# Reordering the opening of a fused attention and mixture-of-experts layer: weight loads, first scores, output-weight folding and the transposes' queue

## The reference, cut to what matters

```python
q_latent = hidden_states @ Wqa
q = (q_latent @ Wqb).reshape(b, s, H, Q_HEAD_DIM)
kv_comp = hidden_states @ Wkva
c_kv, k_pe = (kv_comp[..., :KV_LORA], kv_comp[..., KV_LORA:])
...
kv = (c_kv @ Wkvb).reshape(b, s, H, NOPE_DIM + V_DIM)
scores = jnp.einsum('bhqd,bhkd->bhqk', q_full, k_full) * scale
probs = jax.nn.softmax(jnp.where(causal, scores, min), axis=-1)
attn = jnp.einsum('bhqk,bhkd->bhqd', probs, v)
x = x + attn.reshape(b, s, H * V_DIM) @ Wo
...
y = jnp.einsum('eti,eih,te->th', swiglu(x @ w_gate_up), w_down, combine)
x = x + y + swiglu(x @ shared_gate_up) @ shared_down
```

## Time and profile before

| what | value |
|---|---|
| runs | 1592.03, 1595.13, 1594.93 us |
| the profiled execution | 1592.03 us, of which 1589.2 us is the span of its instructions |
| PE busy | 1463.6 us (92%) |
| DVE / ACT / POOL busy | 1210.4 / 1009.7 / 988.4 us (76 / 64 / 62%) |
| mean granted TensorE clock | 0.982 of full |
| DMA | 144.66 MB, mean 91 GB/s |

### The profile page before, as it was taken

One profiled execution on the slowest core, in us unless ns is written; L12 is line 12 of the kernel. 1 busy time (PEld: TensorE's weight loads), 2 busy tenths in 40 slices (PEclk: granted clock), 3 DMA queues, 4 the chain that ended last, 5 costly groups with the idle time before them and its releaser, 6 DMA issues.

```text
span 1589.2 us, 44790 instructions
## 1 busy us (share of the span) xinstructions
PE 1463.6 (92%) x16413; PEld 1082.6 (68%) x16414; DVE 1210.4 (76%) x2657; ACT 1009.7 (64%) x2399; POOL 988.4 (62%) x1567
## 2 busy tenths in 40 slices
PE   9879999998899999998999999989999999979990
PEld 3557777776667777776677777766777767657770
DVE  6877778987778887877777778877777788556666
ACT  3666667666567666765676667666666666547770
POOL 4477755452878556576878678758786582444450
PEclk9999999999999999999999999999999999989995
DMA  7456933313554331234543123254532311448518
GB/s 214 83 113 162 167 71 67 60 20 71 100 104 74 71 61 31 50 66 84 109 88 71 35 53 65 46 93 78 99 64 42 65 27 31 107 126 249 148 58 320
DMA packets 331075, 144.66 MB, mean 91 GB/s; under 512 B 278546, under 2 KB 321589, under 8 KB 330872
## 3 DMA queue, kind: packets, MB, share of 16 engines
q1 hardware_dynamic: 305296, 104.57, 33.0%
q10 hardware_dynamic: 18664, 20.52, 4.5%
q0 software_dynamic: 6912, 16.83, 3.5%
HBM read 47.04 MB, written 29.53 MB: 48 GB/s over the span
## 4 chain that ended last, share of the span: by engine, by line
PE 70%; DVE 9%; ACT 6%; DMA 5%; issue 4%; SPq 1%; another core or an unknown queue 1%; POOL 1%; ACTq 0%; DVEq 0%; POOLq 0%
PE of_ps L772 28%; PE s_ps L772 25%; PE t_ps L969 15%; DMA qT<-work 3%; DVE pT L1828 2%; ACT probs L1304 2%; ACT pT L1179 1%; ACT work L1182 1%; DVE smax L1801 1%; DVE weights L2037 1%; PE of_ps L1094 1%; PE t_ps L1080 1%; DMA work<-y_exp 1%; DVE work L1625 1%
## 5 line engine op out<-in xcount | busy, mean ns | idle before, releaser
L1828 DVE TENSOR_TENSOR pT<-t_ps,pT 128x512 f16<-128x512 f32 (+3 forms) x688 | 411.0, 598 | 146.6 <-ACT pT L1179 138.4
L1179 ACT CAST pT<-t_ps 128x512 f16<-128x512 f32 (+3 forms) x688 | 355.6, 517 | 239.3 <-PE t_ps L969 238.5
L772 PE MATMUL s_ps<-kT,qT 128*128 128x512 f16 (+3 forms) x2112 | 473.0, 336 | 4.0 <-DMA qT<-work 4.0
L969 PE MATMUL t_ps<-id,probs 128*128 128x128 f32 x2304 | 378.7, 279 | 22.3 <-ACT probs L1304 8.5
L969 PEld LDWEIGHTS t_ps<-id,probs 128*128 128x128 f32 x2304 | 256.9, 141 | 105.9 <-issue 46.4
L772 PEld LDWEIGHTS of_ps<-ckv,pT 128*128 128x128 f16 x6912 | 241.0, 98 | 41.3 <-DVE o_sb L1657 9.5
L772 PE MATMUL of_ps<-ckv,pT 128*128 128x64 f16 x6912 | 257.8, 193 | 7.1 <-DVE o_sb L1657 6.5
L772 PEld LDWEIGHTS s_ps<-kT,qT 128*128 128x128 f16 x2112 | 202.8, 98 | 72.7 <-DMA qT<-work 4.9
L1304 ACT ACTIVATE probs<-s_ps,nmax 128x640 f32<-128x640 f32 (+3 forms) x256 | 245.9, 961 | 0.1
L772 PE MATMUL of_ps<-weights,xT 128*128 128x128 f16 (+1 forms) x930 | 198.0, 349 | 19.0 <-DVE work L1625 8.6
L1790 DVE TENSOR_REDUCE nmax<-s_ps 128x1 f32<-128x640 f32 (+3 forms) x200 | 192.4, 962 | 17.4 <-PE s_ps L772 16.9
(11 more groups left out here) (243 smaller groups left out, 2352.6 us busy)
## 6 DMA issues: line engine op xcount, KB each, us to landing
wgu_sb<-wgu ACTq DMA_DIRECT2D x8, 704.0 KB, 5.1
work<-lists SPq DMA_DIRECT2D x40, 128.5 KB
qT<-lists SPq DMA_DIRECT2D x40, 128.5 KB
x<-x SPq DMA_DIRECT2D x32, 128.0 KB
dense<-den SPq DMA_DIRECT2D x32, 128.0 KB
weights<-dense ACTq DMA_DIRECT2D x1, 4096.0 KB
qT<-y_exp SPq DMA_DIRECT2D x16, 256.0 KB, 6.4
work<-y_exp SPq DMA_DIRECT2D x16, 256.0 KB, 8.2
```

Of the source, the lines that this page charges most:

```text
L772: return pe_.matmul(o, a, b, start=start, stop=stop)
L969: last = pe_.transpose(t_ps[:, h, c * P:(c + 1) * P], probs[:, u % 2, g * L + j * P:g * L + (j + 1) * P], id32[:, :])
L1179: return act.copy(o, i)
L1828: dve.tensor_tensor(pT[:, u % 2, 1, h, 0:w], t_ps[:, h, 0:w], pT[:, u % 2, 0, h, 0:w], ALU.subtract).then_inc(s.lo_p, 1)
```

## The change

1. Loads and semaphores: the semaphore `consts` is gone; its seven loads and those of the cosine and sine tables count one semaphore `c_in`. SP issues the loads in the same order as before.
2. ACT issues the loads of `wvT` and `wo` at its start, as soon as the weights counted by `w_k` have landed, and not after the transposes of input tiles 0 and 1.
3. `constants()` moves on DVE from the end of `row_bounds()` to behind `query_lo(0, 0)`; DVE's own wait for the tables ahead of `latent_lo(0)` is gone.
4. PE: `fold_out(0)`, a wait for `c_ready`, three `busy_id` and the first unit of tile 0's scores come ahead of `project(0, "q1")`; `fold_out(1)` comes behind it and `fold_out(2)` behind `project(1, "q1")`; six `busy_id` instead of four stand ahead of the second unit of scores. The output weights' banks are 2, 2, 0, 0 and not 2, 0, 2, 0, with waits to match.
5. ACT: `out_weights(0)` moves ahead of `rope_hi(1)` and `query_hi(0, 1)`, `out_weights(1)` between the last two `query_hi`, `out_weights(2)` ahead of the first exponentials. DVE: `maxima(0, 0)` moves behind `query_lo(1, 1)`.
6. SP: the transposes are issued in the order keys 0, queries (0, 0), (0, 1), keys 1, queries (1, 0), (1, 1), first keys. Before, the first keys stood third, between the halves of tile 0's queries.

```diff
-        OUT_BANKS = [2, 0, 2, 0]
+        OUT_BANKS = [2, 2, 0, 0]
...
+            dest_in = dest_f[:, :]
             for dst, src in ((id32[:, :], ident), (probs[:, 1, 0:P], causal), (probs[:, 0, 0:P], tri),
                              (iota_e_sb[:, :], iota_e), (iota_k_sb[:, :], iota_k), (iota_p_sb[:, :], iota_p),
-                             (dest_f[:, :], tok_ids)):
-                load(dst, src, s.consts)
-            load(r_nopeT, wqb_nopeT, s.w_k)
-            load(r_wkT, wkT, s.w_k)
-            load(cos_sb[:, :, :], cos_t, s.c_in)
-            load(sin_sb[:, :, :], sin_t, s.c_in)
+                             (dest_in, tok_ids), (cos_sb[:, :, :], cos_t), (sin_sb[:, :, :], sin_t)):
+                load(dst, src, s.c_in)
+                if dst is dest_in:
+                    load(r_nopeT, wqb_nopeT, s.w_k)
+                    load(r_wkT, wkT, s.w_k)
...
-            turn_keys(0)
-            turn_half_queries(0, 0)
+            for n in range(2):
+                turn_keys(n)
+                for g in range(2):
+                    turn_half_queries(n, g)
             turn_first_keys(0)
-            turn_half_queries(0, 1)
-            turn_keys(1)
-            turn_half_queries(1, 0)
-            turn_half_queries(1, 1)
...
             project(1, "q0", 0, 512)
+            fold_out(0)
+            pe_.wait_ge(s.c_ready, 1)
+            busy_id(s_ps[:, 0, :], 3)
+            for h in range(2):
+                scores(0, 0, h)
             pe_.wait_ge(s.lo_made, FIRST)
             project(0, "q1", 512, 512)
-            pe_.wait_ge(s.c_ready, 1)
-            for h in range(2):
-                scores(0, 0, h)
+            fold_out(1)
             project(1, "q1", 512, 512)
-            for pair in range(3):
-                fold_out(pair)
-            busy_id(s_ps[:, 3, :], 4)
+            fold_out(2)
+            busy_id(s_ps[:, 3, :], 6)
             for h in range(2):
                 scores(0, 1, h)
+
+            pe_.wait_ge(s.wo_copied, 3)
             fold_out(3)
-
-            pe_.wait_ge(s.wo_copied, 3)
...
             copy(den[:, 0:1], pT[:, 0, 0, 0, 0:1])
+
+            act.wait_ge(s.w_k, 16 * 2)
+            load(r_wvT, wvT, s.w_o)
+            load(r_wo, wo.rearrange("(h d) n -> d h n", d=VD), s.w_o)
...
-            for k in range(2):
-                act.wait_ge(*x_turned(k))
-            load(r_wvT, wvT, s.w_o)
-            load(r_wo, wo.rearrange("(h d) n -> d h n", d=VD), s.w_o)
...
+            out_weights(0)
+            rope_hi(1)
             query_hi(0, 1)
-            rope_hi(1)
             query_hi(1, 0)
+            out_weights(1)
             query_hi(1, 1)
-            out_weights(0)
-            out_weights(1)
+            out_weights(2)
             exps(0, 0, 0)
-            out_weights(2)
...
-                dve.wait_ge(s.consts, 16 * 7)
+                dve.wait_ge(s.c_in, 16 * 9)
...
                 dve.sem_inc(s.rows_ready, 1)
-                constants()
...
-            dve.wait_ge(s.c_in, 16 * 2)
             latent_lo(0)
...
             query_lo(0, 0)
+            constants()
             lo_parts(7, 8)
...
             query_lo(1, 0)
-            maxima(0, 0)
             query_lo(1, 1)
...
             dve.sem_inc(s.side_free, len(OPENING))
+            maxima(0, 0)
             maxima(0, 1)
```

More of the change, by code:

```diff
@@ L271, in build @@
         s_flat = s_ps[:, :, :].rearrange("p a n -> p (a n)")
-        names = """c_in consts w_k w_a0 w_a1 w_o w_kv w_b filled c_ready qb_made qb_copied wq_made wo_made wo_copied prep
+        names = """c_in w_k w_a0 w_a1 w_o w_kv w_b filled c_ready qb_made qb_copied wq_made wo_made wo_copied prep
                    rows_ready row_sums amax_ready scales hi_made lo_made w_d
@@ L822, in fold_out @@
                     pe_.wait_ge(s.w_o, 16 * 2)
-                if pair < 2:
+                if pair % 2 == 0:
                     k = OUT_BANKS[pair]
@@ L827, in fold_out @@
                 else:
-                    pe_.wait_ge(s.wo_copied, pair - 1)
+                    pe_.wait_ge(s.wo_copied, pair)
                 bank = early_banks[OUT_BANKS[pair]]
```

## The result

The changed kernel takes 1603.37 us, the median of five runs (1602.24 to 1605.74), against 1592.42 us (1591.05 to 1595.13) for the kernel before beside it. The ratio is 1.0069, with a 95% interval of 1.0052 to 1.0087: slower by 11 us. The profiled execution took 1604.73 us with a span of 1602.6, 13.4 us more than the span before.

A forecast was written before the change was run, and what follows sets the result against it. PE was taken to bound the kernel (busy 92% of the span, heading the chain). Terms 2.4 + 2.4 + 3.1 = +7.9 us, added to the three-run mean of 1594.1, gave 1602 us; range 1596 to 1607.

The forecast's parts named there:

- the forecast's own path: Opening of the kernel: parts 2, 3 and 4 add 2.4, 2.4 and 3.1 us, giving 1602 us; chance 0.42.
- the third rival, the lowered clock: PE behind the longer stalls: two new 3 us stalls may each bring half clock, +2.6 to +5 us on top; chance 0.10.
- three signs of being wrong: Input tile 0 lands in under 3 us; last transposes drain faster than SP's 5.67 us for two; other low clock stretches.
- Part 1: Semaphores and moved constants() on DVE: nothing, as the later project(0, "q1") hides it; without that cover 0.5 us.
- Part 2: ACT's early output-weight loads slow input tile 0's transpose, PE stalls 3.2 us, project(0, "q0") starts +2.4 us later.
- The rival of packets taking turns: Input tile 0's transpose beside the early load: landing after 4.3 us, +0.6 instead of +2.4 us; load-slows-little chance 0.25.
- The -0.8 us end of part 2: Lower end with an undisturbed transpose: rotary path and DVE's split 0.9 us earlier, PE uses its gap, -0.8 us.
- Part 3: PE's new order, query half 1 later: 1.5 us wait ahead of tile 0's second scores, section(0) +2.4 us.
- Part 4: First keys last on SP: they land at about 57, PE stalls ahead of tile 1's first scores, +3.1 us.
- the fourth rival: Half-speed stretch at 70 us goes as work arrives in another rhythm: its price is 2.6 us, at most 3.4; chance 0.09.

The follow-up runs named there:

- half load: Kernel before with wvT and the first half of wo (1.5 MB) loaded at ACT's start, the second half in the old place; ratio 1.0000.
- late loads: Changed kernel with the loads of wvT and wo back behind the first two input transposes; ratio 1.0054, median 1600.42 against 1593.35.
- single edits: Kernel before with early loads (1.0028, 1.0029) or first keys last (1.0021); changed kernel with loads and SP's order as before (1.0036).
- filling the gaps: Changed kernel with unread matmuls, 18 ahead of the first projection and 12 ahead of tile 1's first scores; ratio 1.0061.

## Why the prediction was right, point by point

Forecast were +7.9 us for the profiled opening and 1602 us; measured were 12.2 us up to the projection of tile 2, 11 us between the medians, and 1603.4 us. The time was met more closely than the shift, and that is luck: the 7.9 us were added to a mean of 1594.0 us over three runs (the prediction wrote 1594.1), and the kernel before came to 1592.42 beside the changed one. What ran was the forecast's own path and, on top of it, the third rival, the lowered clock, which had been given 0.10: 7.9 + 3.8 = 11.7 us, against 12.2 in the trace. Of the three signs of being wrong that the prediction named one did come, low stretches of the clock that the kernel before does not have (0.53 from 25 to 30 us).

- **Part 1, constants at nothing:** right for this change, where the split they delay has its cover (no gap ahead of `project(0, "q1")` in the changed kernel). The price without the cover was mis-sized: 0.5 us forecast, 1.8 us more gap in the trace and 2.9 us in time, since in its new place the work takes twice as long (3.3 us and 1.6).
- **Part 2, +2.4 us:** the mechanism was right, the term was mis-sized, 5.6 us in the trace. Two of its numbers failed. The landing was taken at 6.1 us as an upper bound and was 7.2: tile 2's transpose had been issued between the two loads (22.39, with `wvT` at 22.34 and the 2 MB of `wo` at 22.70), and tile 0's stood behind both. This cost little, since the transpose was also issued 0.7 us earlier than taken: the first projection began at 23.93 and not 23.4. And the gap was thought to cost only itself; instead the clock fell behind it, and from the first projection to `project(0, "q0")` it took 13.5 us and not 10.7, which is the 2.8 us. That stood among the rivals with a chance of 0.10.
- **The rival of packets taking turns** (a landing of 4.3 us, +0.6): refuted by the queues' packets and by landings that follow the load whenever the transpose was issued; the half load's 0.7 us would have fitted it. The Trainium skill's rule ("DMA: Bandwidth & Descriptors", queues, rings and completion order) describes the engines once both queues have packets there, and after 21 us the rows do show both. What it does not cover is that the transpose's packets came to the engines only when less than a quarter of the load ahead was left; which stage before the engines holds them is not shown by any run.
- **The -0.8 us end of part 2**, the gap ahead of `project(0, "q0")` closed by a freer ACT: not shown. Several kernels have no such gap whatever ACT does.
- **Part 3, +2.4 us:** 2.4 in the changed kernel (8.1 less 5.6), 2.9 with late loads. Right, though two small errors cancel: the gap ahead of the second scores was 1.08 us where 1.5 was forecast, and PE's work from `project(0, "q1")` up to it 6.3 us where 5.9 was.
- **Part 4, +3.1 us:** 3.1 (11.2 less 8.1), a gap of 2.96 us, released by the first keys. Right, and alone it is 2.1. The prediction's own terms (54.5 + 2.4 against 54.0) give 2.9, and not the 3.1 that it wrote.
- **The lowered clock, +2.6 to +5:** it came in addition to the forecast, 2.8 and 1.0 us. The prediction gave them a case of their own. But the three longest gaps (4.24, 3.98 and 2.96 us) were each followed by a stretch of half clock, so with stalls as long as forecast the fall belonged into the forecast. Below that the length of the gap does not decide: 2.21 us, and gaps of 1.85, 2.37 and 2.39 us ahead of the first fold, were followed by a mean granted clock of 0.51 to 0.74, gaps of 1.97 and 1.98 us, and one of 2.29 us ahead of the first fold, were not, and the same 2.14 us were four times out of twelve.
- **The half-speed stretch at 70 us that might go** (the fourth rival): it did not. In the changed kernel it stands from about 88 us (0.60 in 88 to 92, 0.57 in 70 to 78 before), and from tile 2's projection to the first `weights,oT` product it took 22.2 us and 21.8 before.

The single edits cost 0.28 to 0.29%, 0.21% and 0.36% by themselves, 0.85 together, against 0.69% for the whole, within the intervals. What was not shown: why the profiled span ends 13.4 us later and not 12.2 (other stretches of half clock come and go between executions); that undoing part 2 or part 4, or filling the gaps, makes the changed kernel faster in time (each of these differences is within the noise, and what is said of them rests on the traces); and what decides whether the clock falls behind a gap of about 2 us.

## What to carry to other kernels

Before moving a bulk load ahead, look at which small transfer with a waiting engine is issued while it drains: here it stood behind the load until less than a quarter of it was left, even from another queue, and a load cut to what drains in time cost nothing. In an in-order transfer queue put a transfer whose input is ready into the idle stretch, and not behind the last one, however late it is needed. Price a new stall of some 3 us of TensorE with the half-speed stretch behind it: here 4.2 us of gap cost 2.8 more, and 3.0 us cost 1.0. And set a forecast's shift against the measured shift, not only its time against the measured time: the starting value can hide a missing term.

## What the hardware showed unexpectedly

- A transpose on SP's queue sent no packet for over 3 us while a load that ACT had issued before drained (1377 packets against none from 16 to 20 us). Alone it began after 1.2 us.
- A DVE cast of 128x128 float32 values took 1.59 us beside POOL's product, with the constants moved, and 0.23 us in the kernel before, where POOL ran only tiny instructions. POOL's product had begun just before it (38.40 us, the cast at 38.47), and both ended together (40.06 us and 39.98 us). The Trainium skill ("SBUF — State Buffer", section on who interferes with whom) says that a DVE instruction in a fast mode (a cast can be one) and a GpSimd one lock each other out of a port that they share, for a whole instruction; the row agrees.
- The clock also fell without a gap: in the kernel with the constants moved its mean was 0.50 from 16 to 20 us, where PE folded float32 weights for 4.00 of 4 us, after 3.79 of 4 in the stretch ahead. Its 12.23 us in the table's first column, against 10.7 in most kernels, have this cause.
- The start of a run varies: the fold of the first weights began at 5.24 to 7.74 us and took 7.3 to 10.1 us in the profiled executions, and the first projection, where no gap stood ahead of it, came at 19.9 to 24.7 us.
